# The attention output product of a Mamba block in three 16-bit terms, and a new order of work at the batch boundary

## The reference, cut to what matters

```
x = input @ Wx.T;  z = input @ Wz.T;  x = silu(causal_conv4(x))
b, c = x @ Wb.T, x @ Wc.T;  dt = softplus(x @ Wdt.T + b_dt)
y = scan(x, b, c, dt, a) + d_param * x
yn = (y - mean) / sqrt(var + eps)      # mean and var over ALL 1024 tokens and the 64 of a head
out = (yn * gn_w + gn_b) * silu(z);  attn = out @ Wout.T
x = x + layernorm(attn);  x = x + layernorm(ffn(layernorm(x)))
```

## Time and profile before

| | |
|---|---|
| median of 3 runs | 1347.39 us (1345.3 to 1349.34) |
| profiled execution, its own time | 1347.9 us |
| its span | 1346.2 us |
| mean granted TensorE clock | 0.982 of full speed |
| busy: PE, PEld, DVE, ACT, POOL | 94%, 60%, 78%, 56%, 36% |

### The profile page before, as it was taken

One profiled execution on the slowest core, in us unless ns is written; L12 is line 12 of the kernel. 1 busy time (PEld: TensorE's weight loads), 2 busy tenths in 40 slices (PEclk: granted clock), 3 DMA queues, 4 the chain that ended last, 5 costly groups with the idle time before them and its releaser, 6 DMA issues.

```text
span 1346.2 us, 27890 instructions
## 1 busy us (share of the span) xinstructions
PE 1265.5 (94%) x10616; PEld 809.9 (60%) x10616; DVE 1055.1 (78%) x2462; ACT 750.2 (56%) x1270; POOL 485.2 (36%) x559
## 2 busy tenths in 40 slices
PE   6899999999999999999999999999999999999676
PEld 3564657565575756656575665757567565766554
DVE  5574797879888797878978788887978789786575
ACT  5554574556745485554745567454755547455321
POOL 2030444224351434325433243514443154332633
PEclk9998999999999999999999999999999999999788
DMA  7010000101000010101001010010101000010100
GB/s 224 1 49 1 17 0 2 48 1 48 1 22 27 2 48 1 48 1 44 6 1 48 1 48 1 17 32 2 48 1 48 1 30 4 1 33 1 33 1 31
DMA packets 30564, 32.89 MB, mean 24 GB/s; under 512 B 1856, under 2 KB 28628, under 8 KB 30432
## 3 DMA queue, kind: packets, MB, share of 16 engines
q1 hardware_dynamic: 30432, 31.11, 7.3%
HBM read 22.72 MB, written 8.39 MB: 23 GB/s over the span
## 4 chain that ended last, share of the span: by engine, by line
PE 69%; DVE 19%; issue 5%; POOL 4%; ACT 2%; POOLq 0%; DVEq 0%; ACTq 0%
PE bank L1425 25%; PE bank L1619 8%; PE bank L1606 7%; PE bank L1537 5%; PE bank L1591 4%; DVE xs L1067 4%; PE bank L1515 4%; PE bank L1573 3%; PE bank L1560 2%; PE bank L1551 2%; PE bank L1507 2%; DVE un L1042 2%; PE bank L1435 2%; DVE gn_stats L1203 1%; DVE sh L1072 1%
## 5 line engine op out<-in xcount | busy, mean ns | idle before, releaser
L790 POOL TENSOR_TENSOR Cd<-Cd,CT 128x512 f32<-128x512 f32 x64 | 81.4, 1271 | 366.2 <-ACT Cd L987 366.0
L1425 PE MATMUL bank<-sh,WbT 128*128 128x512 f16 x768 | 177.1, 387 | 10.5 <-DVE sh L1072 10.5
L1425 PE MATMUL bank<-sh,WcT 128*128 128x512 f16 x768 | 175.9, 379 | 0.0
L1067 DVE SCALAR_TENSOR_TENSOR xs<-xi,vectors,xs 128x512 f32<-128x512 f32 x192 | 152.5, 803 | 7.7 <-ACT xs L893 3.4
L1425 PEld LDWEIGHTS bank<-sh,WbT 128*128 128x128 f16 x768 | 74.2, 99 | 101.7 <-issue 15.0
L1591 PE MATMUL bank<-WoutT,yT 128*128 128x256 f32 x512 | 118.5, 389 | 12.6 <-POOL yT L767 6.5
L977 ACT ACTIVATE mt<-bank 128x512 f32<-128x512 f32 x128 | 69.6, 600 | 108.1 <-PE bank L1507 108.1
L1425 PEld LDWEIGHTS bank<-sh,WcT 128*128 128x128 f16 x768 | 75.2, 98 | 86.5
L1606 PE MATMUL bank<-uh,sign1T 128*128 128x512 f16 x512 | 121.5, 383 | 2.0 <-DVE uh L1268 2.0
L1619 PE MATMUL bank<-sign2T,hh 128*128 128x256 f16 x1024 | 120.3, 277 | 1.8 <-DVE hh L1279 1.8
L1009 ACT ACTIVATE hf<-bank,vectors,alpha 128x512 f32<-128x512 f32 x128 | 99.5, 777 | 37.9 <-PE bank L1606 26.4
(11 more groups left out here) (196 smaller groups left out, 2453.5 us busy)
## 6 DMA issues: line engine op xcount, KB each, us to landing
xt<-L_attn_input_tensor_dram SPq DMA_DIRECT2D x16, 512.0 KB, 5.0
u<-L_attn_input_tensor_dram SPq DMA_DIRECT2D x16, 512.0 KB, 4.0
out_dram<-u SPq DMA_DIRECT2D x16, 512.0 KB, 3.0
yT<-in_L_ffn_w_dram SPq DMA_DIRECT2D x2, 512.0 KB, 9.7
u<-in_L_ffn_w_dram SPq DMA_DIRECT2D x2, 512.0 KB, 9.5
BT<-in_L_attn_Wx_dram SPq DMA_DIRECT2D x1, 512.0 KB, 4.8
BT<-in_L_attn_Wz_dram SPq DMA_DIRECT2D x1, 512.0 KB, 5.7
zs<-in_L_attn_Wb_dram SPq DMA_DIRECT2D x1, 512.0 KB, 5.3
```

The source lines that it names most:

```text
L790: pool.tensor_tensor(Cd[n % 2][:, :, :], Cd[n % 2][:, :, :], CT[:, :, q * P:(q + 1) * P], ALU.mult)\
L1067: nc.vector.scalar_tensor_tensor(out=xs[:, c, :], in0=xi[:, c, k:k + BLK], scalar=taps[:, c, k:k + 1], in1=xs[:, c, :], op0=ALU.mult, op1= ...
L1425: mm = nc.tensor.matmul(bank(t, key)[:, :], w[i][:, k, cols(m)], v[h][:, k, :], start=(a == 0), stop=(a == len(terms) - 1))
```

## The change

The Wo product becomes 16-bit in three terms. `WoutT` is two 16-bit tiles, scaled by 256, whose low half VectorE makes during setup. After the gate, `yT` is split by new steps `gated`: high on ScalarE, low on VectorE, into `yg`, which lies in the tile `hh` of the feed-forward part. For block 0 these are 4+4 ops of 256 columns on each of the two engines; for block 1, 2+2 ops of 512 columns, placed at the end of the scan of the next batch's block 0. The gate of the second quarter moves from GpSimd to VectorE. The order at the batch boundary is new; the last layernorm is done in two halves at other places, `end_stat` and `head_stat(j, 0)` come earlier in the scan, and the Silu table is loaded at the end of the scan.

```
             steps += own(("xi", 0, 0), ("xi", 0, 1), ("xi", 0, 2)) + tail(("head_stat", NJ - 1, 1), ("gn_sum",), ("gn_mean",))
             steps += own(("xi", 0, 3), ("conv", 0, 0), ("silu", 0, 0), ("xs_hi", 0, 0)) + tail(("gn_root",))
             steps += own(("conv", 0, 1, 0, 2), ("z", 0, 0)) + tail(("gn_fold",)) + own(("conv", 0, 1, 2, 3), ("z", 0, 1))
             steps += tail(("gate", 0, 0), ("gated", 0, 0)) + own(("xs", 0, 0), ("silu", 0, 1), ("xs_hi", 0, 1), ("conv", 0, 2))
             steps += own(("z", 0, 2), ("z", 0, 3)) + tail(("gate", 0, 1), ("gated", 0, 1)) + own(("xs", 0, 1), ("conv", 0, 3))
             steps += tail(("Wo", 0, 0)) + own(*[("z_in", 0, c) for c in range(KI)])
             for c in (2, 3):
                 steps += own(("silu", 0, c), ("xs_hi", 0, c), ("xs", 0, c))
             steps += own(("z_silu",)) + tail(("Wo", 0, 1))
...
-        steps += own(("carry", j, 0), ("ends", j, 1)) + [(who, "in_norm", nj)] + tail(("O", j, 1)) + own(("back", j, 0), ("front", j, 2), ("score", j, 2))
-        steps += own(("carry", j, 1), ("ends", j, 2), ("back", j, 1)) + tail(("end_stat", j)) + own(("front", j, 3), ("score", j, 3))
-        steps += [(who, "xT", nj, 0)] + own(("carry", j, 2), ("ends", j, 3), ("back", j, 2)) + [(who, "xT", nj, 1)]
-        steps += tail(("end_root", j), ("end_norm", j)) + own(("carry", j, 3), ("back", j, 3), ("head_stat", j, 0))
+        norm = [(who, "in_norm", nj)]
+        steps += own(("carry", j, 0), ("ends", j, 1)) + (own(("back", j, 0)) + norm if first else norm + tail(("O", j, 1)) + own(("back", j, 0)))
+        steps += own(("front", j, 2)) + tail(("end_stat", j))
+        steps += own(("score", j, 2), ("carry", j, 1), ("ends", j, 2)) + tail(("end_root", j)) + own(("back", j, 1), ("head_stat", j, 0))
+        steps += own(("front", j, 3), ("score", j, 3)) + [(who, "xT", nj, 0)] + tail(("end_norm", j, 0))
+        steps += tail(("gated", 1, 0)) if j == 0 else []
+        steps += own(("carry", j, 2), ("ends", j, 3), ("back", j, 2)) + [(who, "silu_table"), (who, "xT", nj, 1)] + tail(("end_norm", j, 1))
+        steps += tail(("gated", 1, 1)) if j == 0 else []
+        steps += own(("carry", j, 3), ("back", j, 3))
...
-        WoutT = sb("WoutT", [P, KI, D])
+        WoutT = [sb(f"WoutT{i}", [P, KI, D], F16) for i in range(2)]
...
+        yg = [[v[:, j * KI:(j + 1) * KI, :] for v in hh] for j in range(NJ)]
...
+            def gated_high(t, j, m):
+                s, sj = before_block(t, j) if j == 0 or ring_of(t, ("O", 0, 0)) is not final else (t.ago(1), NJ - 1)
+                act.wait_ge(*full(s, ("O", sj, NQ // 2 - 1)))
+                for c in range(0 if j else KI):
+                    at = slice(m * BLK // 2, (m + 1) * BLK // 2)
+                    act.wait_ge(*g_out.count(t, m * KI + c + 1))
+                    nc.scalar.activation(yg[j][0][:, c, at], yT[:, c, at], ACT.Copy, scale=SY).then_inc(yg_hi.sem, 1)
+                for c in range(2 * m, 2 * m + 2 if j else 0):
+                    act.wait_ge(*g_late.count(t, KI + c + 1))
+                    nc.scalar.activation(yg[j][0][:, c, :], yT[:, c, BLK:T], ACT.Copy, scale=SY).then_inc(yg_hi.sem, 1)
...
             def gate(t, j, m):
 
-                for c in range(0 if j or m else KI):
-                    at = slice(0, BLK // 2)
-                    dve.wait_ge(*yn_out.count(t, c + 1))
+                for c in range(0 if j else KI):
+                    at = slice(m * BLK // 2, (m + 1) * BLK // 2)
+                    dve.wait_ge(*yn_out.count(t, m * KI + c + 1))
                     nc.vector.tensor_tensor(yT[:, c, at], yT[:, c, at], zs[:, c, at], ALU.mult).then_inc(g_out.sem, 1)
+
+            def gated_low(t, j, m):
+                for c in range(0 if j else KI):
+                    at = slice(m * BLK // 2, (m + 1) * BLK // 2)
+                    dve.wait_ge(*yg_hi.count(t, m * KI + c + 1))
+                    nc.vector.scalar_tensor_tensor(out=yg[j][1][:, c, at], in0=yT[:, c, at], scalar=SY, in1=yg[j][0][:, c, at],
+                                                   op0=ALU.mult, op1=ALU.subtract).then_inc(yg_lo.sem, 1)
+                for c in range(2 * m, 2 * m + 2 if j else 0):
...
-                pe.wait_ge(*(g_late.count(t, gated * KI) if gated else g_out.count(t, KI)))
+                pe.wait_ge(*yg_lo.count(t, 3 * KI if j else (m + 1) * KI))
                 pe.wait_ge(*empty(t, key))
                 for i in (2 * m, 2 * m + 1):
-                    for c in range(KI):
-                        mm = nc.tensor.matmul(bank(t, key)[:, (i % 2) * D:(i % 2 + 1) * D],
-                                              yT[:, c, (j * NQ + i) * P:(j * NQ + i + 1) * P], WoutT[:, c, :],
-                                              start=(c == 0), stop=(c == KI - 1))
+                    terms = [(c, w, v) for c in range(KI) for w, v in ((0, 0), (1, 0), (0, 1))]
+                    for a, (c, w, v) in enumerate(terms):
+                        mm = nc.tensor.matmul(bank(t, key)[:, (i % 2) * D:(i % 2 + 1) * D], yg[j][v][:, c, cols(i)],
+                                              WoutT[w][:, c, :], start=(a == 0), stop=(a == len(terms) - 1))
```

More of the change, by code:

```diff
@@ L235, in last_tail @@
     steps = [("head_stat", NJ - 1, 1), ("gn_sum",), ("gn_mean",), ("gn_root",), ("gn_fold",)]
-    steps += [("gate", j, m) for j in range(NJ) for m in range(2)]
-    steps += [("Wo", 0, 0), ("Wo", 0, 1), ("mid_stat", 0), ("mid_norm", 0), ("ff_stat", 0), ("ff_norm", 0)]
+    steps += [("gate", 0, 0), ("gated", 0, 0), ("gate", 0, 1), ("gated", 0, 1), ("gate", 1, 0), ("gate", 1, 1)]
+    steps += [("Wo", 0, 0), ("Wo", 0, 1), ("mid_stat", 0), ("gated", 1, 0), ("gated", 1, 1), ("mid_norm", 0), ("ff_stat", 0), ("ff_norm", 0)]
     steps += [("Wo", 1, 0), ("Wo", 1, 1), ("mid_stat", 1), ("uT", 0), ("mid_norm", 1), *hidden(0, 0, 4)]
@@ L569, in opening @@
             return isinstance(t.b, int) and t.b + t.d == 0
-        lows = [key for key in turns if key[0] in ("Wx", "Wz", "Wb", "Wc", "Wdt")]
-        signs = [key for key in turns if key[0] in ("Wout", "w2", "w1")]
+        lows = [key for key in turns if key[0] in ("Wx", "Wz", "Wb", "Wc", "Wdt", "Wout")]
+        signs = [key for key in turns if key[0] in ("w2", "w1")]
         setup_read = {key: (low_set, n + 1) for n, key in enumerate(lows)}
@@ L763, in gate @@
                 n = 2 * j + m
-                for c in range(KI if n else 0):
+                for c in range(KI if j else 0):
                     at = slice(n * BLK // 2, (n + 1) * BLK // 2)
@@ L853, in weights @@
                     elif name == "Wout":
[L854 to L855 removed]
+                        nc.scalar.activation(WoutT[0][:, 2 * k:2 * k + 2, :], w.rearrange("p (k n) -> p k n", k=2), ACT.Copy,
+                                             scale=SW).then_inc(w_split, 1)
                     elif name == "w2":
@@ L1013, in _ @@
                 "weights": weights, "silu_table": table(ACT.Silu), "gelu_table": table(ACT.Gelu), "xT": input_high, "xi": project_x,
-                "z_in": gate_in, "z_silu": gate_silu, "silu": x_silu, "xs": x_high, "dt": step_exp,
+                "z_in": gate_in, "z_silu": gate_silu, "silu": x_silu, "xs_hi": x_high, "dt": step_exp,
                 "log": step_log, "cums": cum_top, "skip": skip_term, "C": project_c, "decays": decay_exp, "front": front, "ends": ends,
-                "gate": head_normalise, "uT": middle_high, "H": hidden})
+                "gate": head_normalise, "gated": gated_high, "uT": middle_high, "H": hidden})
         @block.vector
@@ L1021, in _, with statistics @@
                       dt_step, da_seen, cum_split, cum_roles, ends_made, mt_out, xdt_out, st_out, yT_out, gn_st, gn_mo, gn_step, g_out,
-                      mid_out, un_out, uh_lo, hh_hi, hh_lo, y2_scaled, y2_norm):
+                      yg_lo, mid_out, un_out, uh_lo, hh_hi, hh_lo, y2_scaled, y2_norm):
                 s.prime(dve)
-            def statistics(w, t, j, tile, ready):
+            def statistics(w, t, j, tile, ready, eps=EPS):
                 for i in range(NQ):
@@ L1247, in middle_stats @@
                 statistics("mid", t, j, lambda i: attention_tile(t, j, i),
-                           lambda i: dve.wait_ge(*full(t, ("Wo", j, i // 2))))
+                           lambda i: dve.wait_ge(*full(t, ("Wo", j, i // 2))), EPS * (SW * SY) ** 2)
             def middle_norm(t, j):
@@ L1294, in end_stats, with end_norm @@
                            lambda i: dve.wait_ge(*y2_out.count(t, j * NQ // 2 + i // 2 + 1)))
-            def end_norm(t, j):
-                for i in range(NQ):
+            def end_norm(t, j, m=None):
+                for i in range(NQ) if m is None else range(2 * m, 2 * m + 2):
                     v = ffn_buffer(t, j)[:, i, :]
@@ L1307, in weights @@
                         dst, w = [v[:, :, :] for v in WdtT], w[:, 0:KI * HEADS].rearrange("p (k h) -> p k h", k=KI)
+                    elif name == "Wout":
```

(3 more changed lines are left out.)

53 lines of the change are left out of this document (29 added, 24 removed).

## The result

The changed kernel takes 1365.1 us (median of four runs, 1364.4 to 1366.0) against 1348.4 for the kernel before: ratio 1.0132, 95% interval 1.0120 to 1.0145. It is slower, as forecast, but by 17 us and not by 5, and 1 us outside the range. (Single executions of two kernels further down ran at a granted clock of 0.75 from end to end, in 1614 and 1617 us, and are left out of their times.)

A forecast was written before the change was run, and what follows sets the result against it. VectorE's work was taken to bound the batch boundary, TensorE's order the rest. Boundary +1.9 and block 1's turn -0.1, taken as +1.5 a batch, gave +10.5 over seven, less 5.6 once: 1347.9 to 1353 us, range 1343 to 1364.

The forecast's parts named there:

- TensorE's saving: Wo products: 48 16-bit matmuls at 0.109 each take 5.25 us, so -1.65 us per block in a stream without waits.
- The scan, both blocks: Chunk 2 of each scan: earlier `end_stat` delays `mt`, so `ends` on TensorE starts 0.90 us later, twice per batch.
- Block 0's scan, second half: Chunk 3's state product waits a further 0.65 us for `state`, behind half a layernorm and two `gated` ops on VectorE.
- port rival: Block 0's scan: `gated` ops slowed beside GpSimd, +0.4 us each, +0.8 a batch, 1358 us; chance 0.13.
- Block 1's turn: Mid-batch, from block 0's scan into block 1: delays of 0.90 and 0.65 against 1.65 saved, -0.1 us a batch.
- The batch boundary: Turn between batches: VectorE's added and removed work nets +1.9 us; TensorE waits 2.1 and 3.2 us for low halves.
- Clock, rival 1: Batch boundary: waits of 2.1 and 3.2 us drop TensorE's clock, 7 x 1.2 = +8 us, 1361 us; chance 0.22.
- Once per run: First batch -2.8 us from two removed waits; last tail -2.5 and -0.3; together -5.6 us.
- The sum: Whole run: +1.8 us a batch, taken as +1.5, seven times +10.5, less 5.6, gives +4.9 and 1353 us.

## Why the forecast was wrong, step by step

The profiled times go from a span of 1346.2 to 1363.4 us: -7.0 up to the first head sums, +24.4 over seven batches, -0.2 behind the last. Forecast were -2.8, +10.5 and the rest of -5.6.

- *TensorE's saving.* Right: block 1's 48 matmuls take 5.24 us before the next product starts (5.25), 1.66 less, and block 0's buys nothing.
- *The scan, both blocks.* Right in mechanism and size: `ends` of chunk 2 waits 0.68 for `mt`, and the stretch is 0.85 and 0.87 longer (0.90).
- *Block 0's scan, second half.* The step that failed: "it waits a further 0.65". It waits 1.81, and 0.53 more follow before the second group of block 1's input product; the stretch is 2.4 us longer. Of the difference to 0.65, 1.1 is the first pair of low halves, taken at 0.62 each where GpSimd stands beside them. And 0.4 is the wrong releaser: I took `state`, which is over by 396.49, while the bank waits for the first `yT` addition behind it, and the product starts at 396.93. (That is 0.3 more than was missing; the work ahead of them was that much quicker than I had it.) The second pair, 1.1 over its price, gives the 0.53. Moving these operations took both waits away: 1.65 us less a batch between batches at full clock, 2.6 where the clock had fallen behind the wait. It is the port rival's mechanism, at twice its price (1.1 and 0.53 against +0.8). The Trainium skill (SBUF — State Buffer, Who interferes with whom) has a VectorE instruction with two SBUF inputs and a GpSimd instruction that reads SBUF exclude each other for their whole length; the 1.76 us beside `Cd` agrees with that, and the forecast cited it and then gave it 0.13.
- *Block 1's turn: -0.1.* It is 0.85 + 2.4 - 1.66 = +1.6. With the cut of the sum from +1.8 to +1.5 below, this is the whole miss of a batch at full clock.
- *The batch boundary.* Right: +1.7 (1.9), with waits of 1.88 and 2.72 (2.1 and 3.2), convolutions from 0.92 to 0.77 and the 0.61 for `state` gone. Block 0's product is the larger part of it, 1.5 a batch (159.18 against 157.65 above). The reduction of the sum from +1.8 to +1.5 a batch, for stalls that "may partly coincide with gaps", was not borne out.
- *Clock, rival 1.* True in two batches of seven, so +3 us and not +8, and less than half of it at the boundary, where the rival had it. In a batch like 800.58 to 962.97 the boundary is 0.64 longer than at full clock; the other 0.9 comes in block 0's scan, where in the same two batches the clock falls again, behind the 1.81 us wait (0.61 from 880 to 884 us). So the wait that was mis-sized also cost clock. The second half product in one of them, in the timeline and by its window (the clock at its lower level, 1.2 GHz):

```profile
814.86 4.24 PE L1626 MATMUL bank<-WoutT,hh 128*128 128x256 f16 x24 [2.72 <-DVE hh L1268]
```

```profile
816.50:819.50 3.00, 3.00 (x15) 1.98 (x13) 2.21 (x4) 2.33 (x5) 0.00 (x0) 0.51 0.00 0
```

- *Once per run.* The first batch gained 7.0 instead of 2.8. I counted the two waits of 3.5 us, not the clock: before, it was at its lower level, 1.2 GHz, from 106 to 116 us, and now for about 4 of these 10 us. Six microseconds at full instead of half clock are 3 us of work, an estimate that leaves 1.2 of the 4.2 unexplained. Windows of the kernel before and then of the kernel after:

```profile
106.00:116.00 10.00, 8.93 (x66) 3.81 (x67) 3.94 (x10) 4.70 (x7) 0.00 (x0) 0.50 0.01 2
```

```profile
106.00:110.00 4.00, 3.58 (x35) 1.62 (x34) 1.77 (x3) 1.75 (x2) 0.00 (x0) 0.57 0.01 4
110.00:116.00 6.00, 6.00 (x53) 3.04 (x50) 2.79 (x14) 1.74 (x3) 0.00 (x0) 1.00 0.00 0
```

  The last batch grew by 2.0 where the others grew by 3.1 to 3.3, so it gained 1.2 (the wait for head moments is 3.54, not 6.46), where -2.5 was forecast.
- *The sum.* In place of +1.5 a batch stand 1.7 + 1.6 = +3.3 (+23 over seven), the clock's +3, and less in the last batch; the first batch's 4 us more than forecast hid part of it.

What stays open: why the same 24 matmuls behind the same wait of 2.73 us ran at full clock in one batch and at half in the next. Also, that the low halves at 0.62 would have left a wait of 0.7 was not shown: in the run where the first pair stood in the same place and was that quick (1.28 for two, statistics behind chunk 1) other work had moved ahead of it, and the wait was 2.1.

## What to carry to other kernels

Before an operation is put into an engine's queue, look at what stands behind it, to the end of the readers of each bank that the other engine takes next: a bank is free when its last reader is done, not when the one that was looked at is. Price an added VectorE operation by a row in which GpSimd does what it will do beside it, not by the fastest row of its kind. And when a change brings an order of its own, time order and product apart: here the two useful moves of the order were worth 10 to 12 us with the old product and were hidden by the rest. Read the clock of each batch before two kernels are compared by their batches: a move that seemed to be worth 2.6 us a batch was 1.65 of waits and 0.9 of clock.

## What the runs showed of the hardware

- A VectorE operation of two SBUF inputs (128x512, 32 bits to 16) took 0.68 us alone, 1.21 beside GpSimd's additions, and 1.76 when it met a GpSimd multiplication of 1.31 us at its start. Beside a GpSimd operation of 128x4 (1.38 us, last tail) it stayed at 0.68.
- Behind a wait of 2.72 or 2.73 us, 24 matmuls took 2.79 us in some batches and 4.2 to 4.5 in others of one execution. Behind 1.69 to 1.89 us the same 24 took 2.79 in all fourteen batches of the changed kernel and of the run with the low halves behind the scan. But behind the 1.81 us wait in block 0's scan the clock fell in two batches of seven of the changed kernel, and in six of seven with block 1's product alone.
- An instruction issued later in the program on an engine with an empty queue starts no later: GpSimd's additions stood directly behind its last `state` operation in both places.
